# A 4096-row weighted table sum with its two matmul operands exchanged, and its result scaled straight out of PSUM

## The chip, the cores and the metric

The kernel runs on one core of one Trainium2 chip. The metric is device time in microseconds of one execution, median of three runs.

## The reference

The reference is a small audio network on x of shape (128, 256, 64): a depthwise convolution with normalisation, a bilinear attention, a product-key memory layer with causal attention, a linear attention, and a mixture of eight experts. The change touches the memory layer alone. For each of 128 tokens and 8 heads it scores 2 x 64 sub-keys, takes the best 16 of the 4096 sums, and adds up table rows with softmax weights:

```
final_scores, pk_idx = jax.lax.top_k(score, FINAL_TOPK)
final_indices = jnp.take_along_axis(index, pk_idx, axis=-1)
final_scores = jax.nn.softmax(final_scores, axis=-1)
k = jnp.einsum('bnhk,bnhkd->bnhd', kv_scores, keys_table[ind])
v = jnp.einsum('bnhk,bnhkd->bnhd', kv_scores, values_table[ind])
```

A table row is 128 wide here, 64 numbers of the key beside 64 of the value.

## The kernel before, in words

The batch of 128 is worked off as 64 pairs. Three heads of eight are gathered: GpSimd fetches the 16 rows of a token by indirect DMA and VectorE weighs them. The other five heads are dense: all 4096 rows of the head's table take part, each with the weight exp(score) or zero. The 4096 rows are 32 chunks of 128, so a pair has 5 x 32 = 160 chunks, called beats.

Chunks go in twos. For two chunks TensorE runs `ranks` (L1414, two f16 matmuls into a bank `p_s`), ScalarE cuts off what is not chosen (L1169), TensorE adds the exponents (`exponents`, L1423), ScalarE writes exp of the bank into `ew` (L1174), a tile of 128 table rows x (2 batches x 128 tokens). Nine beats later (`LAG`) `product` (L1436) multiplies: the table chunk (128 rows x 128) is the weight operand, the 256 columns of `ew` stream past it, and the sum over 32 chunks grows in bank `p_d` as (128 table columns) x (256 tokens). One f32 matmul call is two weight loads and two matmul instructions in the trace.

When a head's 32 chunks are in, `empty` (ScalarE, L1180) copies `p_d` to SBUF (`dense_t_sb`) and so frees it; the next head's first product waits for that. Some beats later `cross` (TensorE, L1443) transposes both batches' halves into bank `p_g`, and `keep_dense` (ScalarE, L1188) scales each by `fin_r`, one factor per token, and writes it to `kv`.

`p_g` is shared: three times per head `prepare` fills it (L1378, L1388, L1397) with the maps of a later head, ScalarE copies each fill to `mov` (L1158, L1160), and the transposes are the fourth user. All users count one semaphore, `bank_free`; `bank_use` works out at which count each may begin.

Every engine runs its own instructions strictly in a written order. Each piece of work (front, select, prep, tail, back, weigh, sums, dense) is a generator that yields due times in beats, and `interleave` always emits the piece that is due first. In one period the dense heads of a pair run beside `back` of the pair before (attention, linear attention, experts), `select` of the pair ahead, and `front` of the one after that. `BACK` spreads the steps of `back` evenly from `TAIL_END + 1` to beat 155. A period has 80 twos of chunks. Lines used below: L1521 is probabilities times values, L1542 to L1544 the query, key and value products of the linear attention, L1554 its product with `l1_a` (VectorE, L996), L1559 its output product with the expanded `prob_t` (VectorE, L1001), L1277 the ScalarE logarithm of the last variance `b_var` (VectorE, L1027). VectorE's L915 and L922 build one-hot rank tiles of 128x2048 and 128x1024, L943 adds gathered rows.

Of the kernel before, what the change touches and what calls it, by code (L numbers as in the profile page):

```python
# [21 lines left out]
PAIRS = B // 2  # L22
# [72 lines left out]
TAIL_END = LAG + 6  # L95
# [68 lines left out]
def after_dense(d):  # L164

    ready = CHUNKS * (d + 1) + LAG
    return ready + 0.7, ready + 3.25

BANK_ORDER = [k for _, k in sorted([(after_dense(d)[1] % BEATS, ("dense", d)) for d in range(DENSE)]
                                   + [(at_fill(d, i), ("map", 3 * d + i))
                                      for d in range(DENSE) for i in range(3)])]


def bank_use(pair, kind, k):


    at = BANK_ORDER.index((kind, k))  # L180
    period = pair.n + (kind == "dense" and k == DENSE - 1) - (kind == "map" and k < 3)
    before = 2 + len(BANK_ORDER) * period + at
    if not isinstance(period, int):
        return before
    if period < 0:
        return k
    if period == 0:
        return before + (at <= BANK_ORDER.index(("dense", DENSE - 1)))
    if period == PAIRS - 1:
        return before - sum(BANK_ORDER.index(("map", i)) < at for i in range(3))  # L190
    return 2 + len(BANK_ORDER) * period - 3 if period == PAIRS else before

# [12 lines left out]
def over_pairs(eng, front, select, prep, tail, back, weigh, sums, dense):  # L205
# [3 lines left out]
    def period(own, before, ahead, later):  # L209
# [11 lines left out]
        if own is not None:  # L221
            chains += [weigh(own), sums(own), dense(own)]
# [19 lines left out]
def build(nc, x, rows, conv_m, attn_w_src, wqpk_t, keys_t, wq, table, wo, wqkv, wout, wr, w1, b1_t, w2, dense_t, out):  # L242
# [107 lines left out]
    dense_t_sb = sb("dense_t_sb", [128, 2 * T])  # L350
# [111 lines left out]
    dense_tr = sem("dense_tr")  # L462
# [203 lines left out]
    def _(dve):  # L666
# [423 lines left out]
        over_pairs(dve, front, select, prep, nothing, back, weigh, nothing, nothing)  # L1090

    @block.scalar
    def _(act):
# [83 lines left out]
        def empty(pair, d):  # L1177

            act.wait_ge(product_done, BEATS * pair.n + CHUNKS * (d + 1))
            A.copy(dense_t_sb[:, :], p_d[:, 0:2 * T]).then_inc(dense_out_ready, 1)  # L1180

        def keep_dense(pair, d):
            if d == 0:
                act.wait_ge(kv_w_ready, pair.n + 1)
            act.wait_ge(dense_tr, DENSE * pair.n + d + 1)
            for p in range(2):
                g = HEADS * p + GATHERED + d
                last = A.activation(kv[pair.par][:, p, :, GATHERED + d, :],  # L1188
                                    p_g[:, 128 * p:128 * p + 128].rearrange("t (s c) -> t s c", s=2), ACT.Copy,
                                    scale=fin_r[pair.par][:, g:g + 1])  # L1190
            last.then_inc(bank_free, 1)

        def dense(pair):
            for u in range(TWOS):
# [6 lines left out]
                if d > 0 and past == 0:  # L1201
                    yield after_dense(d - 1)[0]
                    empty(pair, d - 1)

        def tail(pair):
            yield BEATS - 2 + EXP_AT - BEATS
            exponent(pair, TWOS - 1)
            yield after_dense(DENSE - 1)[0] - BEATS
            empty(pair, DENSE - 1)
            yield after_dense(DENSE - 1)[1] + 1.15 - BEATS  # L1210
# [4 lines left out]

        def sums(pair):
            for kind, k in BANK_ORDER:
                if kind == "dense" and k < DENSE - 1:
                    yield after_dense(k)[1] + 1.15
                    keep_dense(pair, k)  # L1220
# [75 lines left out]
        over_pairs(act, front, select, prep, tail, back, nothing, sums, dense)  # L1296

    @block.tensor
    def _(pe):
# [66 lines left out]
        def prepare(pair, d):  # L1366
            def fill(part):
                use = bank_use(pair, "map", 3 * d + part)
                if positive(use):
                    hold(pe, bank_free, use)  # L1370
# [35 lines left out]
        def ranks(pair, u):  # L1406
            d, k = divmod(2 * u, CHUNKS)
            if k == 0:
                hold(pe, bank_free, bank_use(pair, "map", 3 * d + 2) + 1)
# [17 lines left out]
        def product(pair, c):  # L1427
# [223 lines left out]
```

## Time and profile before

| | us |
|---|---|
| median of 3 runs | 11342.55 (11342.33 to 11344.62) |
| profiled execution, its time | 11344.7 |
| its span, first to last instruction | 11343.0 |
| TensorE matmuls busy | 10198.0 |
| weight loads busy | 8003.0 |
| VectorE busy | 8728.9 |
| ScalarE busy | 7603.9 |
| TensorE idle for ScalarE's L1169 | 275.0 |
| TensorE idle before L1443 | 127.2 |

Busy time is the union of the intervals in which an engine has something under way. A matmul instruction is shown with its whole passage through the array, so back to back matmuls overlap in the record, and the distance from one start to the next tells their price rather than the length of one. In the page a line of the costliest groups gives count, total busy time, mean length of one, and the idle time of the engine just before them with what ended it.

### The profile page before, as it was taken

How to read it: one execution, taken by the hardware profiler on the slowest of the kernel's cores; microseconds unless marked ns; L12 is line 12 of the kernel's file. 1: busy time of each engine (PE TensorE's matmuls, PEld its weight loads, DVE VectorE, ACT ScalarE, POOL GpSimd, SP SyncE). 2: the span in 40 equal slices, each digit the busy share in tenths (PEclk: the TensorE clock that was granted, in tenths of full speed). 3: DMA queues.
4: the chain of work that ended last, by engine and by line, in shares of the span. 5: the costliest groups of instructions: out<-in, count | busy, mean ns of one | idle time of the engine just before them, and what ended most of it. 6: DMA issues, size and time to landing. Idle time of an engine off the chain costs nothing.

```text
span 11343.0 us, 281179 instructions
## 1 busy us (share of the span) xinstructions
PE 10198.0 (90%) x72608; PEld 8003.0 (71%) x72608; DVE 8728.9 (77%) x41793; ACT 7603.9 (67%) x17491; POOL 6186.2 (55%) x6186
## 2 busy tenths in 40 slices
PE   5998989989999899999998999999999989989998
PEld 4777767777777677777777777777777777777776
DVE  7877778778777787787777877777778778777783
ACT  4666666666666666666666666666666666666665
POOL 5555555555555555555555555555555555555553
PEclk9999999999999999999999999999999999999998
DMA  2333333333333333333333333333333333333332
GB/s 77 100 99 98 100 97 100 100 97 101 99 99 101 97 101 98 99 100 98 99 99 99 100 98 99 99 99 98 99 100 99 99 99 99 99 99 98 99 99 69
DMA packets 603820, 1108.58 MB, mean 98 GB/s; under 512 B 158672, under 2 KB 175568, under 8 KB 602192
## 3 DMA queue, kind: packets, MB, share of 16 engines
q1 hardware_dynamic: 405328, 686.35, 19.0%
q0 software_dynamic: 196608, 403.05, 14.2%
q8 instruction: 714, 11.70, 0.4%
q14 instruction: 882, 7.23, 0.2%
q10 hardware_dynamic: 288, 0.27, 0.0%
HBM read 1084.90 MB, written 4.19 MB: 96 GB/s over the span
## 4 chain that ended last, share of the span: by engine, by line
PE 54%; DVE 19%; ACT 15%; issue 7%; DVEq 4%; ACTq 1%; POOL 0%; DMA 0%; POOLq 0%
PE p_d L1436 20%; PE p_s L1414 6%; PE p_g L1378 5%; PE p_s L1423 5%; ACT ew L1174 4%; ACT p_s L1169 3%; DVE gath L943 3%; PE p_f L1362 2%; ACT prob L1242 2%; PE p_x L1585 2%; PE p_x L1521 2%; PE p_x L1578 2%; DVE rank_hot L915 1%; PE p_x L1507 1%; PE p_x L1514 1%
## 5 line engine op out<-in xcount | busy, mean ns | idle before, releaser
L654 POOL DMA_INDIRECT gath<-in_table,idx x6144 | 6161.9, 1003 | 5033.8 <-PE p_d L1436 3894.5
L1436 PE MATMUL p_d<-ew,tab 128*128 128x256 f32 x20480 | 5715.2, 390 | 11.5 <-ACT dense_t_sb L1180 4.2
L1169 ACT ACTIVATE p_s<-p_s 128x512 f32<-128x512 f32 x5120 | 3053.4, 596 | 2677.1 <-PE p_s L1414 2638.4
L1436 PEld LDWEIGHTS p_d<-ew,tab 128*128 128x128 f32 x20480 | 3411.4, 193 | 377.3 <-issue 46.5
L1174 ACT ACTIVATE ew<-p_s 128x512 f32<-128x512 f32 x5120 | 3077.0, 601 | 151.1 <-PE p_s L1423 149.6
L1423 PE MATMUL p_s<-mov,piece_sel 128*128 128x256 f16 x10240 | 1966.1, 274 | 284.8 <-ACT p_s L1169 275.0
L1414 PE MATMUL p_s<-mov,rank_sel 128*128 128x256 f16 x10240 | 1972.7, 275 | 47.2 <-issue 38.2
L1414 PEld LDWEIGHTS p_s<-mov,rank_sel 128*128 128x128 f16 x10240 | 966.1, 100 | 830.7 <-issue 279.4
L943 DVE SCALAR_TENSOR_TENSOR gath<-gath,kv_w 128x128 f32<-128x128 f32 x4608 | 1310.4, 346 | 64.2
L1423 PEld LDWEIGHTS p_s<-mov,piece_sel 128*128 128x128 f16 x10240 | 956.8, 98 | 533.2 <-issue 397.9
L915 DVE TENSOR_TENSOR rank_hot<-iota_k,rank_key 128x2048 f16<-128x2048 f16 x640 | 777.2, 1223 | 84.7 <-issue 72.1
L1378 PEld LDWEIGHTS p_g<-ident_rank,rank_hot 128*128 128x128 f16 x10240 | 675.6, 103 | 174.2 <-issue 96.6
L1378 PE MATMUL p_g<-ident_rank,rank_hot 128*128 128x128 f16 x10240 | 731.2, 229 | 50.0 <-ACT kv L1188 45.6
L755 DVE MAX8 top<-sim 128x8 f32<-128x64 f32 x2048 | 291.6, 212 | 569.1 <-ACT sim L1144 568.0
L922 DVE TENSOR_TENSOR rank_hot<-rank_hot,rank_val 128x1024 f16<-128x1024 f16 x640 | 424.3, 688 | 29.4 <-issue 0.9
L763 DVE FIND_INDEX8 top_i<-top,sim 128x8 uint32<-128x64 f32 x2048 | 410.1, 219 | 0.0
L785 DVE FIND_INDEX8 top_i<-top,sim 128x8 uint32<-128x64 f32 x2048 | 407.4, 219 | 2.3 <-issue 0.3
L938 DVE TENSOR_SCALAR gath<-gath,kv_w 128x128 f32<-128x128 f32 x1536 | 340.1, 291 | 83.3 <-DMA gath<-in_table,idx 68.3
L771 DVE MATCH_REPLACE8 sim<-top,sim 128x64 f32<-128x64 f32 x2048 | 403.0, 208 | 0.0
L1242 ACT ACTIVATE prob<-p_x,neg_max 128x128 f32<-128x128 f32 x1024 | 385.6, 409 | 13.5 <-DVE neg_max L962 13.5
L1160 ACT CAST mov<-p_g 128x512 f16<-128x512 f32 x640 | 391.4, 611 | 1.4 <-PE p_g L1388 0.8
L1362 PE MATMUL p_f<-score_w,xh_t 64*128 64x512 f32 x512 | 290.1, 647 | 32.4 <-ACT xh_t L1140 30.0
(238 smaller groups left out, 12024.7 us busy)
## 6 DMA issues: line engine op xcount, KB each, us to landing
tab<-in_dense_t SPq DMA_DIRECT2D x2560, 256.0 KB
gath<-in_table,idx POOLq DMA_INDIRECT x6144
xin<-in_x SPq DMA_DIRECT2D x64, 128.0 KB, 2.2
out<-h_out SPq DMA_DIRECT2D x64, 64.0 KB
row_consts<-in_rows SPq DMA_DIRECT2D x1, 548.0 KB, 4.5
w_sb<-in_w SPq DMA_DIRECT2D x1, 512.0 KB, 6.2
w_sb<-in_w ACTq DMA_DIRECT2D x1, 256.0 KB, 4.8
gath<-in_wqpk_t SPq DMA_DIRECT2D x1, 256.0 KB, 5.7
```

Source lines behind the costliest of these rows:

```text
L654: G.indirect_dma_start(out=gath[:, slot, k, :], out_offset=None, in_=table[:, :], in_offset=bass.IndirectOffsetOnAxis(ap=idx[pair.par][:, ...
L915: V.tensor_tensor(hots[p].rearrange("t r s c i -> t (r s) c i"), iota_k[:, :].rearrange("t (c i) -> t c i", i=2)[:, None, :, :].to_broadca ...
L922: V.tensor_tensor(hots[p][:, :, 0, :, :], hots[p][:, :, 0, :, :], rank_val[:, DENSE * p + d, :, None, :].to_broadcast([T, TOPK, SUBKEYS // ...
L943: V.scalar_tensor_tensor(rows[:, k, :], rows[:, first + k, :], share[:, first + k:first + k + 1], rows[:, k, :], ALU.mult, ALU.add)
L1169: A.activation(bank[:, :], bank[:, :], ACT.Relu, scale=-STEEP).then_inc(penalty_ready, 1)
L1174: A.activation(ew[:, slot:slot + 2, :].rearrange("m c t -> m (c t)"), p_s[u % PS_RING][:, :], ACT.Exp, scale=-1.0).then_inc(weights_ready, 1)
L1242: last = A.activation(prob[:, a, hp, :], px[:, a, T * hp:T * hp + T], ACT.Exp, bias=neg_max[:, h:h + 1], accum_out=row_sum[:, a, hp:hp + 1])
L1362: M(p_f[:, :], xh2_t[pair.par][lanes(p), :], score_w[lanes(p), 512 * s:512 * s + 512], start=True, stop=True).then_inc(sim_mm, 1)
L1378: last = M(p_g[:, T * p:T * p + T], rank_hot[p][:, r, :, :].rearrange("t s i -> t (s i)"), ident_rank[:, r, :], start=(r == 0), stop=(r == ...
L1414: last = M(p_s[u % PS_RING][:, 2 * T * i:2 * T * i + 2 * T], rank_sel[:, k + i, :], mov[mov_slot(d)][:, 0, :], start=(i == 0), stop=False, ...
L1423: last = M(p_s[u % PS_RING][:, 2 * T * i:2 * T * i + 2 * T], piece_sel[:, k + i, :], mov[mov_slot(d)][:, MAP_OF[layout], :], start=False, ...
L1436: M(p_d[:, 0:2 * T], tab[:, u % TAB_RING, i, :], ew[:, c % EW_RING, :], start=(k == 0), stop=(k == CHUNKS - 1)).then_inc(product_done, 1)
```

## The change

The operands of the dense product are exchanged. The weight operand is now `ew`, 128 table rows x 128 tokens of one batch, and the table chunk with its 128 columns streams past it. So there is one call per batch, two calls per chunk, each with 128 moving columns; the semaphore is raised once per chunk as before. `p_d` then holds (128 tokens) x (2 batches x 128 table columns), which is the orientation of `kv`. `keep_dense` scales out of `p_d` into `kv` at the place where `empty` stood, and its last instruction is what the next head's first product waits for. `empty`, `cross`, the generator `sums`, `dense_t_sb`, the semaphore `dense_tr` and the transposes' turns in `p_g` are gone. `TAIL_END` becomes `LAG + 2`, so `back` starts four beats earlier and its steps are spread over 143 beats instead of 139.

```diff
-TAIL_END = LAG + 6
+TAIL_END = LAG + 2
 def after_dense(d):
-    ready = CHUNKS * (d + 1) + LAG
-    return ready + 0.7, ready + 3.25
+    return CHUNKS * (d + 1) + LAG + 0.7
+def fills_before(pair, d, part):
+    return 3 * DENSE * pair.n + 3 * d + part
...
-        def empty(pair, d):
-            act.wait_ge(product_done, BEATS * pair.n + CHUNKS * (d + 1))
-            A.copy(dense_t_sb[:, :], p_d[:, 0:2 * T]).then_inc(dense_out_ready, 1)
-
         def keep_dense(pair, d):
             if d == 0:
                 act.wait_ge(kv_w_ready, pair.n + 1)
-            act.wait_ge(dense_tr, DENSE * pair.n + d + 1)
+            act.wait_ge(product_done, BEATS * pair.n + CHUNKS * (d + 1))
             for p in range(2):
                 g = HEADS * p + GATHERED + d
                 last = A.activation(kv[pair.par][:, p, :, GATHERED + d, :],
-                                    p_g[:, 128 * p:128 * p + 128].rearrange("t (s c) -> t s c", s=2), ACT.Copy,
+                                    p_d[:, KV * p:KV * p + KV].rearrange("t (s c) -> t s c", s=2), ACT.Copy,
                                     scale=fin_r[pair.par][:, g:g + 1])
-            last.then_inc(bank_free, 1)
+            last.then_inc(dense_out_ready, 1)
...
             if k == 0 and positive(DENSE * pair.n + d):
                 hold(pe, dense_out_ready, DENSE * pair.n + d)
-            M(p_d[:, 0:2 * T], tab[:, u % TAB_RING, i, :], ew[:, c % EW_RING, :], start=(k == 0),
-              stop=(k == CHUNKS - 1)).then_inc(product_done, 1)
-
-        def cross(pair, d):
-            hold(pe, dense_out_ready, DENSE * pair.n + d + 1)
-            hold(pe, bank_free, bank_use(pair, "dense", d))
-            for p in range(2):
-                last = TR(p_g[:, 128 * p:128 * p + 128], dense_t_sb[:, T * p:T * p + T], ident[:, :])
-            last.then_inc(dense_tr, 1)
+            for p in range(2):
+                last = M(p_d[:, KV * p:KV * p + KV], ew[:, c % EW_RING, T * p:T * p + T], tab[:, u % TAB_RING, i, :],
+                         start=(k == 0 and p == 0), stop=(k == CHUNKS - 1), skip_group_check=True)
+            last.then_inc(product_done, 1)
```

Three places in the engines' orders, first before and then after. Line numbers are those of each kernel: L1436 became L1401 (the product), L1378 became L1342, L1414 L1378, L1423 L1387, L1333 L1298. TensorE from the first product of the next head on, at the end of a pair's second dense head, before:

```order
L1436 MATMUL p_d<-ew,tab 128x256
L513 REGISTER_ALU
L1378 MATMUL p_g<-ident_rank,rank_hot 128x128 x16
L1414 MATMUL p_s<-mov,rank_sel 128x256 x2
L513 REGISTER_ALU
L1423 MATMUL p_s<-mov,piece_sel 128x256 x2
L1436 MATMUL p_d<-ew,tab 128x256 x2
L1333 MATMUL p_f<-f_mv,mean_w 128x2
L513 REGISTER_ALU
L1443 MATMUL p_g<-ident,dense_t_sb 128x128 x2
L1414 MATMUL p_s<-mov,rank_sel 128x256 x2
```

and after:

```order
L1401 MATMUL p_d<-tab,ew 128x128 x2
L491 REGISTER_ALU
L1342 MATMUL p_g<-ident_rank,rank_hot 128x128 x16
L1378 MATMUL p_s<-mov,rank_sel 128x256 x2
L491 REGISTER_ALU
L1387 MATMUL p_s<-mov,piece_sel 128x256 x2
L1401 MATMUL p_d<-tab,ew 128x128 x4
L1298 MATMUL p_f<-f_mv,mean_w 128x2
L1378 MATMUL p_s<-mov,rank_sel 128x256 x2
L491 REGISTER_ALU
L1387 MATMUL p_s<-mov,piece_sel 128x256 x2
```

The transposes are gone from between L1333 and the next ranks, and one product call per chunk has become two of half the width.

ScalarE at the end of the third dense head. Before, with L1169 the cut, L1174 the exponentials, L1180 the copy, L1158 the fill's copy, L1188 the scaling:

```order
L1179 REGISTER_ALU
L1180 COPY dense_t_sb<-p_d 128x256
L1168 REGISTER_ALU
L1169 ACTIVATE p_s<-p_s 128x512
L1174 ACTIVATE ew<-p_s 128x512
L1155 REGISTER_ALU
L1158 ACTIVATE mov<-p_g,rank_off 128x256
L1168 REGISTER_ALU
L1169 ACTIVATE p_s<-p_s 128x512
L1174 ACTIVATE ew<-p_s 128x512
L1185 REGISTER_ALU
L1188 ACTIVATE kv<-p_g,fin_r 128x2x64 x2
```

and after, where L1161 is the scaling, L1147 the cut, L1152 the exponentials and L1136 the fill's copy:

```order
L1158 REGISTER_ALU
L1161 ACTIVATE kv<-p_d,fin_r 128x2x64 x2
L1146 REGISTER_ALU
L1147 ACTIVATE p_s<-p_s 128x512
L1152 ACTIVATE ew<-p_s 128x512
L1133 REGISTER_ALU
L1136 ACTIVATE mov<-p_g,rank_off 128x256
L1146 REGISTER_ALU
L1147 ACTIVATE p_s<-p_s 128x512
L1152 ACTIVATE ew<-p_s 128x512
```

The scaling has moved from two cuts later to the place of the copy.

VectorE some twenty beats later, where `l_a` (L996) and `prob_t` (L1001) are made for TensorE. Before:

```order
L834 TENSOR_TENSOR cand_i<-sim 128x16x4
L913 REGISTER_ALU
L915 TENSOR_TENSOR rank_hot<-iota_k,rank_key 128x2048
L834 TENSOR_TENSOR cand_i<-sim 128x16x3
L834 TENSOR_TENSOR cand_i<-sim 128x16x6
L834 TENSOR_TENSOR cand_i<-sim 128x16x8
L996 SCALAR_TENSOR_TENSOR l_a<-p_x,k_inv,blocks 128x128
...
L853 TENSOR_TENSOR sim<-iota_c,pos_h 128x2496
L922 TENSOR_TENSOR rank_hot<-rank_hot,rank_val 128x16x64 x2
L1001 TENSOR_TENSOR prob_t<-p_x,head_of 128x1024
```

and after (L974 makes `l_a`, L979 makes `prob_t`, L893 and L900 are the rank tiles):

```order
L812 TENSOR_TENSOR cand_i<-sim 128x16x4
L974 SCALAR_TENSOR_TENSOR l_a<-p_x,k_inv,blocks 128x128
L891 REGISTER_ALU
L893 TENSOR_TENSOR rank_hot<-iota_k,rank_key 128x2048
L812 TENSOR_TENSOR cand_i<-sim 128x16x3
L812 TENSOR_TENSOR cand_i<-sim 128x16x6
L812 TENSOR_TENSOR cand_i<-sim 128x16x8
...
L831 TENSOR_TENSOR sim<-iota_c,pos_h 128x2496
L979 TENSOR_TENSOR prob_t<-p_x,head_of 128x1024
L900 TENSOR_TENSOR rank_hot<-rank_hot,rank_val 128x16x64 x2
```

`l_a` now stands ahead of one large rank tile and three candidate adds, and `prob_t` ahead of the two multiplications of the rank tiles. TensorE's L1554 and L1559 themselves stand about one product earlier after the change.

## Rows read from the trace of the kernel before

**Rows 1.** The page of the profiled execution: span, and busy us (share of span) xinstructions.

```profile
span 11343.0 us, 281179 instructions
...
PE 10198.0 (90%) x72608; PEld 8003.0 (71%) x72608; DVE 8728.9 (77%) x41793; ACT 7603.9 (67%) x17491; POOL 6186.2 (55%) x6186
```

**Rows 2.** TensorE groups by line: out<-in shapes xcount | busy us, mean ns | idle before.

```profile
L1436 PE MATMUL p_d<-ew,tab 128*128 128x256 f32 x20480 | 5715.2, 390 | 11.5 <-ACT dense_t_sb L1180 4.2 <-issue 2.1
...
L1521 PE MATMUL p_x<-kv,prob_t 128*128 128x64 f32 x2048 | 246.6, 274 | 2.5 <-ACT prob_t L1248 2.5
...
L1443 PE MATMUL p_g<-ident,dense_t_sb 128*128 128x128 f32 x640 | 127.5, 281 | 127.2 <-ACT mov L1158 126.5 <-ACT dense_t_sb L1180 0.7
```

**Rows 3.** TensorE's waits: who waited for whom, us in total, times, longest.

```profile
PE p_s L1423 <- ACT p_s L1169: 275.0, 315, 2.4
PE p_x L1559 <- DVE prob_t L1001: 129.3, 63, 2.3
PE p_g L1443 <- ACT mov L1158: 126.5, 192, 1.0
PE p_x L1554 <- DVE l_a L996: 105.4, 63, 1.7
...
PE p_g L1378 <- ACT kv L1188: 45.6, 63, 0.8
```

**Rows 4.** Timeline of TensorE at one head's end: start us, us, engine line op.

```profile
5067.55 0.67 PE L1436 MATMUL p_d<-ew,tab 128*128 128x256 f32 x2
5068.06 1.06 PE L1378 MATMUL p_g<-ident_rank,rank_hot 128*128 128x128 f16 x16
5068.95 0.38 PE L1414 MATMUL p_s<-mov,rank_sel 128*128 128x256 f16 x2
...
5069.39 1.03 PE L1436 MATMUL p_d<-ew,tab 128*128 128x256 f32 x4
5070.26 0.28 PE L1333 MATMUL p_f<-f_mv,mean_w 128*128 128x2 f32 x2
5071.43 0.41 PE L1443 MATMUL p_g<-ident,dense_t_sb 128*128 128x128 f32 x2 [0.89 <-ACT mov L1158]
5071.67 0.38 PE L1414 MATMUL p_s<-mov,rank_sel 128*128 128x256 f16 x2
```

**Rows 5.** Timeline of ScalarE over the same stretch.

```profile
5066.55 0.59 ACT L1174 ACTIVATE ew<-p_s 128x512 f32<-128x512 f32 x1
5067.03 0.38 ACT L1180 COPY dense_t_sb<-p_d 128x256 f32<-128x256 f32 x1
5069.37 0.58 ACT L1169 ACTIVATE p_s<-p_s 128x512 f32<-128x512 f32 x1 [1.96 <-PE p_s L1414]
5069.87 0.59 ACT L1174 ACTIVATE ew<-p_s 128x512 f32<-128x512 f32 x1
5070.34 0.30 ACT L1110 ACTIVATE b_log<-b_mv,eps_ln 128x2 f32<-128x2 f32 x1
5070.71 0.20 ACT L1112 ACTIVATE b_rstd<-b_log 128x2 f32<-128x2 f32 x1
5070.82 0.46 ACT L1158 ACTIVATE mov<-p_g,rank_off 128x256 f16<-128x256 f32 x1
5072.09 0.58 ACT L1169 ACTIVATE p_s<-p_s 128x512 f32<-128x512 f32 x1 [0.81 <-PE p_s L1414]
5072.58 0.59 ACT L1174 ACTIVATE ew<-p_s 128x512 f32<-128x512 f32 x1
5073.06 0.63 ACT L1188 ACTIVATE kv<-p_g,fin_r 128x128 f32<-128x128 f32 x2
```

**Rows 6.** Timeline of TensorE, 128-column f32 matmuls back to back.

```profile
5077.60 0.39 PE L1543 MATMUL p_x<-xh_t,wqkv_sb 128*128 128x128 f32 x2
5077.82 0.39 PE L1544 MATMUL p_x<-xh_t,wqkv_sb 128*128 128x128 f32 x2
5078.05 0.60 PE L1436 MATMUL p_d<-ew,tab 128*128 128x256 f32 x2
```

**Rows 7.** Weight loads (PEld) by line, same columns as rows 2.

```profile
L1436 PEld LDWEIGHTS p_d<-ew,tab 128*128 128x128 f32 x20480 | 3411.4, 193 | 377.3 <-issue 46.5
...
L1521 PEld LDWEIGHTS p_x<-kv,prob_t 128*128 128x128 f32 x2048 | 246.7, 194 | 8.1 <-issue 3.4
```

**Rows 8.** VectorE groups of the page: xcount | busy us, mean ns | idle before.

```profile
L943 DVE SCALAR_TENSOR_TENSOR gath<-gath,kv_w 128x128 f32<-128x128 f32 x4608 | 1310.4, 346 | 64.2
...
L915 DVE TENSOR_TENSOR rank_hot<-iota_k,rank_key 128x2048 f16<-128x2048 f16 x640 | 777.2, 1223 | 84.7 <-issue 72.1
...
L922 DVE TENSOR_TENSOR rank_hot<-rank_hot,rank_val 128x1024 f16<-128x1024 f16 x640 | 424.3, 688 | 29.4 <-issue 0.9
```

**Rows 9.** ScalarE's waits.

```profile
ACT b_log L1277 <- DVE b_var L1027: 148.5, 63, 2.6
```

**Rows 10.** Busy us of the engines in three stretches around L1559's wait, granted clock (PEclk).

```profile
5080.00:5098.00 18.00, 13.38 (x83) 10.34 (x80) 16.68 (x64) 11.95 (x27) 13.19 (x12) 1.00 0.42 117
5098.00:5106.30 8.30, 7.99 (x69) 7.17 (x70) 7.68 (x15) 0.37 (x1) 1.59 (x2) 0.59 0.17 49
5106.30:5120.00 13.70, 12.10 (x83) 9.12 (x80) 9.63 (x33) 9.87 (x23) 9.15 (x9) 1.00 0.35 98
```

**Rows 11.** Mean granted clock of the execution.

```profile
core 0: 11343.0 us, clock 0.980
```

More of the change, by code:

```diff
@@ L164, in after_dense @@
 def after_dense(d):
-    ready = CHUNKS * (d + 1) + LAG
-    return ready + 0.7, ready + 3.25
[L172 to L191, printed above, removed]
+    return CHUNKS * (d + 1) + LAG + 0.7
+def fills_before(pair, d, part):
+    return 3 * DENSE * pair.n + 3 * d + part
 def interleave(*chains):
@@ L202, in interleave, with over_pairs @@
         nearest[0] = next(nearest[1], None)
-def over_pairs(eng, front, select, prep, tail, back, weigh, sums, dense):
+def over_pairs(eng, front, select, prep, tail, back, weigh, dense):
     def period(own, before, ahead, later):
@@ L221, in period @@
         if own is not None:
-            chains += [weigh(own), sums(own), dense(own)]
+            chains += [weigh(own), dense(own)]
         interleave(*chains)
@@ L1089, in _ @@
         V_sync()
-        over_pairs(dve, front, select, prep, nothing, back, weigh, nothing, nothing)
+        over_pairs(dve, front, select, prep, nothing, back, weigh, nothing)
     @block.scalar
@@ L1201, in dense @@
                 if d > 0 and past == 0:
[L1202 to L1203 removed]
+                    yield after_dense(d - 1)
+                    keep_dense(pair, d - 1)
         def tail(pair):
@@ L1294, in back @@
             A.preload_act_table_set("natural_log_exp_and_others")
-        over_pairs(act, front, select, prep, tail, back, nothing, sums, dense)
+        over_pairs(act, front, select, prep, tail, back, nothing, dense)
     @block.tensor
@@ L1367, in fill @@
             def fill(part):
-                use = bank_use(pair, "map", 3 * d + part)
-                if positive(use):
-                    hold(pe, bank_free, use)
+                if positive(fills_before(pair, d, part)):
+                    hold(pe, bank_free, fills_before(pair, d, part))
             for p in range(2):
@@ L1464, in tail @@
                 product(pair, c)
-            yield after_dense(DENSE - 1)[1] - BEATS
-            cross(pair, DENSE - 1)
-        def sums(pair):
-            for kind, k in BANK_ORDER:
-                if kind == "dense" and k < DENSE - 1:
-                    yield after_dense(k)[1]
-                    cross(pair, k)
         def back(pair):
@@ L1485, in back @@
             yield BACK["k_tr"]
-            hold(pe, bank_free, bank_use(pair, "dense", DENSE - 1) + 1)
+            hold(pe, dense_out_ready, DENSE * count)
             hold(pe, summed, 2 * GATHERED * count)
@@ L1589, in nothing @@
             return iter(())
-        over_pairs(pe, front, select, prep, tail, back, nothing, sums, dense)
+        over_pairs(pe, front, select, prep, tail, back, nothing, dense)
     ctx.close()
```

13 lines of the change are left out of this document (2 added, 11 removed).

## The prediction

> **What bounds the kernel now.** I read the page first, then TensorE's groups by line, then its waits, then the timeline at a head's end. TensorE has a matmul under way in 10,198 of 11,343 us; no other engine is above 77% [rows 1]. Half of that is the dense product, 5,715 us in L1436 [rows 2]. So time is TensorE's instruction stream plus its 1,145 us of idleness (11,343 − 10,198), and the stream is written in a fixed order, so each wait is one instruction that holds up all behind it. The dearest waits are short and repeat in every pair: for ScalarE's cut 275 us, for two VectorE results 129 and 105, before the transposes 126.5, before a map fill 45.6 [rows 3]. The reader is to see that starts, not lengths, price a matmul: four instructions of L1436 start at 5069.39 and the next line starts at 5070.26, so 0.87 us for four, 0.435 us per call, although each is shown 0.39 long [rows 2, 4].
>
> **The product itself (+150 us).** There are 10,240 calls with 256 moving columns (20,480 instructions), each 0.435 us. After the change there are 20,480 calls with 128 columns: as many columns, but four weight loads per chunk for two. The same shape (f32, 128x128 weights, 128 columns) runs back to back in L1543 and L1544: two instructions from 5077.60 to 5077.82, two more to 5078.05, so 0.225 per call, 0.45 per chunk [rows 6]. That is 0.015 more per chunk, times 10,240: +154, taken as +150. Bounds: L1521, in which 64-column matmuls leave the weight load as the pace, has 246.6 us for 2,048, 0.120 each [rows 2], four make 0.48, +0.047 per chunk, +480 us. From below, sixteen of L1521 in a long run would show a little less than 0.11 apiece when the tail is taken off, which makes the product free: 0. I take [rows 6], since they are this very shape.
>
> A rule of the Trainium skill bears on this. The loads of L1436 are under way 3,411 us for 20,480, 0.167 each [rows 7]. "Perfetto Trace Analysis", section "Identifying the Most-Contended Engine", says that matmul busy time is no good measure and that the busy share of weight loads is to be judged instead. By it the loads, now 71%, would go to 8,003 + 3,411 − 74 = 11,340 us, the whole span, and the change would be bad. The trace agrees only in part: L1521's loads, packed, are under way 0.120 each (246.7 for 2,048), so the 0.167 is stretched by the matmul in front.
>
> **The hand-over of the bank (+60 us).** The next head's first product waits until `p_d` is read. Before, one copy: 5067.03 to 5067.41, and the product starts at 5067.55 [rows 4, 5]. I read the 0.14 as the way of the signal, not as slack. Now the two scalings stand there; as a pair they take 0.63 against 0.38 [rows 5], so the product is 0.25 later. Behind it on TensorE stand sixteen rank matmuls and everything else. Four heads of five look so; in the fifth ScalarE sits idle before the copy and TensorE runs slowly, which I cost at nothing. 256 x 0.25 = +64, taken as +60; if 0.14 were slack 256 x 0.11 = 28; if all five, 80.
>
> **The transposes (−75 us) and their waits (−126 us).** L1443 starts at 5071.43 and the next line at 5071.67: 0.24 a head [rows 4], times 320 = 75 us. Before it TensorE waited 126.5 us in 192 cases, three heads of five, for ScalarE's L1158 to empty the shared bank [rows 3]; the timeline shows why: products end, ScalarE is still at L1169, L1174, two roots and L1158, which starts at 5070.82 and ends at 5071.28 [rows 5]. With no turn of the transposes in the bank, TensorE goes on to ranks, whose bank is free. The next user of the shared bank comes some four calls later.
>
> **The fill that waited for the scaling (−46 us).** L1378 waited 45.6 us, 63 times up to 0.8, for L1188 [rows 3]. L1188 no longer touches that bank. What is late next is the rank tile of VectorE; that is in none of the dear waits, so I take all of it. Bounds of both removed waits: nothing to all.
>
> **What the earlier start of `back` moves (−110 us).** VectorE makes `l_a` now ahead of one L915, 1.22 us [rows 8], and some adds. TensorE waited for it 1.67 us in each pair (105.4 / 63) [rows 3], and arrives a product, 0.43, earlier (my estimate from the order; a call is 0.435): 63 x (1.22 − 0.43) = 50. `prob_t` is ahead of two L922, 1.38 us; the wait was 2.05 us (129.3 / 63); 63 x (1.38 − 0.43) = 60. Bounds: 0, and both waits whole, 235.
>
> **What comes back (+61 us).** In about 20 of the 80 twos, from the key and query products to L1277, VectorE sets the pace (the waits of [rows 3, 9] lie there). Products dearer by 0.015 cost nothing in it: a quarter of 150, −37. But what TensorE gains at `l_a` and `prob_t` is partly met again at L1277, where ScalarE waits 148.5 us for VectorE's `b_var` [rows 9] and holds up the next cut. That wait moves one two earlier on ScalarE (1.31 us of TensorE's time: 0.44 for ranks and exponents from 5068.95 to 5069.39, and 0.87 for two products) [rows 4], while `b_var` loses four L943, 1.38 us, ahead of it. So it stays as long as it is, and I let half of the 110 come back: +55. Of the two removed bank waits (172) I let a quarter return at the cut of L1169: +43.
>
> **The rest.** ScalarE loses 320 copies of 0.38, 121 us of 7,604; it idles a third of the time, so nothing. The gathers and table loads count the same semaphore once per chunk as before: nothing.
>
> **Sum** on the profiled execution: 150 + 60 − 75 − 126 − 46 − 110 + 61 = −86. Its own time is 11,344.7, 1.7 above its span and 2 above the median. 11,342.5 − 86 gives 11,257; I say 11,260.
>
> A second rule would sharpen the first term. Per load and matmul the trace shows 0.112 [rows 6]. "TensorE: Matmul & The Clock Gate", section "LDWEIGHTS (loading the stationary operand)", gives a load as its columns over 1.2 per ns, 107 ns for 128. By it, as an estimate, a chunk would cost 0.427, no more than before, and the sum would end at about 11,100. The measured row decides, and it is 5 ns apiece above it.
>
> **Rivals.**
> - *Everything removed is kept, and the clock stays up.* After the wait for `prob_t` the granted clock falls to its 1.2 GHz level: 0.59 on the mean over 5098.0 to 5106.3, 1.00 on both sides [rows 10]. The whole run has 0.980 [rows 11], so 2% of 11,343, 227 us, of TensorE's time are lost to it. If the shorter waits at L1554 and L1559 keep it at 2.4 GHz in half the pairs, and nothing comes back, the time is 11,260 − 70 − 60 = 11,130. For it: the fall stands right behind the two longest waits. [...] Chance 0.22.
> - *Slower: the waits come back while the loads stay.* A wait for a bank is only where a late ScalarE or VectorE shows. If they are late whatever TensorE does, it meets them one step on, at L1387 (the old L1423), and of the gains only the transposes' own 75 are left: 150 + 60 − 75 − 37 = +98: about 11,440. It decides the sign once more than 184 of the 282 us (126 + 46 + 110) return; 98 are already let back in the forecast. For it: the order of `back` against the fills of the bank has changed, and the eight exponentials of the second attention now start nearer to a head's end, where the scalings are. Against it: ScalarE catches up within a two, 0.97 us from one cut to the end of the exponentials' turn (5069.37 to 5070.34) [rows 5] against 1.30. Chance 0.19.
> - *Loads pace the product at 0.120.* +480 for +150: about 11,590. Against it [rows 6]. Chance 0.04.
> - *No change.* The same, with just those 184 returned: 11,342. Chance 0.11.
>
> **How the numbers follow.** My forecast, with 11,190 to 11,318, has 0.44. What a measurement tells from no change is 0.2%, 23 us. Faster by more: 0.44 + 0.22 and a little of the sum's tails, 0.68. Within: 0.11. Slower: 0.21. The range reaches from the clock rival to nearly the slower one: 11,090 to 11,420.
>
> **What would show it.** Right: L1401 with 40,960 instructions whose fours of calls take 0.90 from start to next start; TensorE idle before it for L1161 or a gap of 0.25 more at each head's first product; no idle of 0.9 between L1298 and L1378; the wait for `l_a` under 60 us in total and for `prob_t` under 80; weight loads under way near 9,200 us and not 11,300. Wrong: waits at L1387 grown by more than 150 us, a start distance of 0.12 per load in L1401, or a mean clock below 0.980.

## The result, and the profile after

The changed kernel takes 11,660.4 us (median of four runs), the one before 11,342.4: ratio 1.0284, interval 1.0266 to 1.0302. I had forecast 11,260 and "faster" at 0.68. It is 2.8% slower, and above my range of 11,090 to 11,420.

The page of the kernel after, its first line and its line of busy times:

```profile
span 11661.2 us, 319239 instructions
...
PE 10409.8 (89%) x92448; PEld 9373.4 (80%) x92448; DVE 8731.9 (75%) x41793; ACT 7583.3 (65%) x17171; POOL 6251.0 (54%) x6186
```

Beside [rows 1] TensorE is busy 212 us more and idle 106 us more. Two groups of part 5, the product's matmuls and its weight loads:

```profile
L1401 PE MATMUL p_d<-tab,ew 128*128 128x128 f32 x40960 | 5961.0, 283 | 131.4 <-ACT kv L1161 122.7
L1401 PEld LDWEIGHTS p_d<-tab,ew 128*128 128x128 f32 x40960 | 5253.4, 196 | 320.6 <-issue 204.1
```

TensorE's waits after (for whom, us in total, times, longest us):

```profile
PE p_x L1454 <- DVE k_t L948: 220.9, 64, 3.5
PE p_x L1510 <- DVE prob_t L979: 158.5, 63, 2.9
PE p_f L1305 <- DVE xh L667: 151.8, 64, 29.9
PE p_d L1401 <- ACT kv L1161: 122.7, 148, 3.1
PE p_s L1387 <- ACT p_s L1147: 121.4, 317, 2.1
PE p_x L1516 <- DVE xn L1015: 88.2, 63, 6.2
...
PE p_x L1505 <- DVE l_a L974: 40.2, 63, 0.7
```

Beside [rows 3] three things went as forecast: no wait is left before transposes, next to none before the map fill (3.3 us for 45.6), and `l_a` fell from 105.4 to 40.2. But one row is new and the dearest of all: 221 us in 64 pairs for `attn_o`, the first attention's result, which lies in the buffer that the rows call `k_t`. Before, it was a wait in one pair, of 0.9 us. (In the same way `prob_t` at L1510 is `l1_x`, the expanded tile of the linear attention.)

Where in a pair the time went, I read by measuring from one pair of rank matmuls to the next (L1414 before, L1378 after), 80 such steps ("twos") a pair, mean over 58 pairs (the fourth to the 61st). A table of sums in us worked out from the traces; the columns beside the first and last are experiments, told below:

```
twos     before  e3     j3     e1     e4    after
0-3       8.47   9.54   8.69   9.20   9.37   9.39
4-7       9.52   9.58   8.62   8.72  10.33  10.34
8-11      8.54   8.65   8.54   8.65   7.03   7.03
12-19    15.66  15.66  15.67  15.66  19.21  22.42
20-24    12.92  13.00  12.74  12.82  11.49  11.81
25-35    22.66  22.82  22.66  22.83  22.14  22.13
36-38     7.33   7.37   6.31   6.38   7.88   7.88
39-47    13.80  14.01  13.80  14.01  13.93  13.95
48-52    17.76  18.20  18.83  17.86  17.85  18.02
53-60    12.54  12.63  11.24  11.46  12.56  12.57
61-70    21.49  21.48  20.46  20.56  20.43  20.32
71-79    23.84  24.12  24.13  24.01  23.98  24.00
pair    174.54 177.07 171.70 172.16 176.20 179.83
```

After against before, +5.3 us a pair, and one stretch holds it: twos 12 to 19 take 6.8 more (earlier work of `back` stands there too, so a part is only moved from later twos). There the timeline of VectorE shows, after:

```profile
5154.51 0.20 DVE L749 MATCH_REPLACE8 sim<-top,sim 128x64 f32<-128x64 f32 x1
5156.93 0.20 DVE L944 RECIPROCAL row_inv<-row_sum 128x8 f32<-128x8 f32 x1 [2.22 <-ACT prob L1207]
5157.28 1.23 DVE L893 TENSOR_TENSOR rank_hot<-iota_k,rank_key 128x2048 f16<-128x2048 f16 x1
...
5158.83 0.60 DVE L758 MAX8 top<-sim 128x8 f32<-128x64 f32 x4
...
5169.53 0.68 DVE L948 TENSOR_TENSOR k_t<-p_x,row_inv 128x512 f32<-128x512 f32 x1
```

and the same place before:

```profile
5017.54 0.21 DVE L771 MATCH_REPLACE8 sim<-top,sim 128x64 f32<-128x64 f32 x1
5017.90 1.23 DVE L915 TENSOR_TENSOR rank_hot<-iota_k,rank_key 128x2048 f16<-128x2048 f16 x1 [0.15 <-issue]
...
5019.44 0.60 DVE L780 MAX8 top<-sim 128x8 f32<-128x64 f32 x4
...
5024.10 0.20 DVE L966 RECIPROCAL row_inv<-row_sum 128x8 f32<-128x8 f32 x1
...
5032.28 0.67 DVE L970 TENSOR_TENSOR k_t<-p_x,row_inv 128x512 f32<-128x512 f32 x1
```

The reader is to see the place of one short instruction. `row_inv`, the reciprocal of the attention's sums, was behind the rank tile, the MAX8s and the weighing of gathered values; when its turn came ScalarE's exponentials were long done. Now it is right behind the MATCH_REPLACE8s, ahead of all that, and VectorE stands idle 2.22 us for ScalarE. Everything behind is late, `attn_o` (L948) last. TensorE at that time, after:

```profile
5166.21 0.61 PE L1401 MATMUL p_d<-tab,ew 128*128 128x128 f32 x4
5170.35 0.59 PE L1454 MATMUL p_x<-causal,ident_bf 128*128 128x512 bf16 x2 [3.53 <-DVE k_t L948]
5170.88 1.82 PE L1458 MATMUL p_x<-k_t,q_t 64*128 64x128 f32 x16
5172.63 1.22 PE L1401 MATMUL p_d<-tab,ew 128*128 128x128 f32 x4
```

And at the same instructions before:

```profile
5033.60 0.38 PE L1423 MATMUL p_s<-mov,piece_sel 128*128 128x256 f16 x2
5033.82 0.59 PE L1503 MATMUL p_x<-causal,ident_bf 128*128 128x512 bf16 x2
5034.35 1.16 PE L1507 MATMUL p_x<-k_t,q_t 64*128 64x128 f32 x16
```

It waits 3.53 us for `attn_o`, and the score products behind it (16 instructions) then take 1.82 us where they took 1.16, and the next four of the product 1.22 where 0.61 is usual: the lower clock. VectorE's own waits, after:

```profile
DVE row_inv L944 <- ACT prob L1207: 673.3, 128, 12.4
DVE top L733 <- ACT sim L1122: 344.0, 128, 8.1
```

Before, the first of these (L966) was 91.4 us. The granted clock over the run is 0.962 (0.980 before, [rows 11]); summed over the trace's stretches at the lower level that is 887 us in place of 463.

### The profile page after: what moved, and what is told of

Same layout as the page of the kernel before. It is cut to its first block, busy times and chain, and to the rows that moved or that the text cites. A ratio compares the mean times of both kernels' runs of the same rounds, so it can differ in the third digit from the quotient of the medians.

```text
span 11661.2 us, 319239 instructions
## 1 busy us (share of the span) xinstructions
PE 10409.8 (89%) x92448; PEld 9373.4 (80%) x92448; DVE 8731.9 (75%) x41793; ACT 7583.3 (65%) x17171; POOL 6251.0 (54%) x6186
## 4 chain that ended last, share of the span: by engine, by line
PE 38%; DVE 34%; ACT 12%; issue 9%; DVEq 7%; ACTq 0%; POOL 0%; POOLq 0%
PE p_d L1401 14%; DVE gath L921 6%; PE p_s L1378 4%; ACT ew L1152 4%; DVE rank_hot L893 3%; PE p_s L1387 3%; PE p_g L1342 3%; ACT prob L1207 3%; ACT p_s L1147 2%; PE p_x L1536 2%; DVE top_i L763 2%; PE p_f L1327 2%; PE p_x L1458 2%; PE p_x L1529 1%; DVEq L923 1%
## 5 line engine op out<-in xcount | busy, mean ns | idle before, releaser
L632 POOL DMA_INDIRECT gath<-in_table,idx x6144 | 6226.8, 1013 | 5287.7 <-PE p_d L1401 4203.9
L1401 PE MATMUL p_d<-tab,ew 128*128 128x128 f32 x40960 | 5961.0, 283 | 131.4 <-ACT kv L1161 122.7
L1401 PEld LDWEIGHTS p_d<-tab,ew 128*128 128x128 f32 x40960 | 5253.4, 196 | 320.6 <-issue 204.1
L1147 ACT ACTIVATE p_s<-p_s 128x512 f32<-128x512 f32 x5120 | 3044.7, 595 | 3263.3 <-PE p_s L1378 3239.8
L1152 ACT ACTIVATE ew<-p_s 128x512 f32<-128x512 f32 x5120 | 3077.5, 601 | 89.2 <-PE p_s L1387 85.3
L1387 PE MATMUL p_s<-mov,piece_sel 128*128 128x256 f16 x10240 | 1994.9, 277 | 121.8 <-ACT p_s L1147 121.4
L1378 PE MATMUL p_s<-mov,rank_sel 128*128 128x256 f16 x10240 | 2000.9, 278 | 43.4 <-issue 35.8
L1387 PEld LDWEIGHTS p_s<-mov,piece_sel 128*128 128x128 f16 x10240 | 981.1, 99 | 360.5 <-issue 227.8
L1378 PEld LDWEIGHTS p_s<-mov,rank_sel 128*128 128x128 f16 x10240 | 987.4, 102 | 312.5 <-issue 247.7
L893 DVE TENSOR_TENSOR rank_hot<-iota_k,rank_key 128x2048 f16<-128x2048 f16 x640 | 776.5, 1222 | 92.8 <-issue 64.9
L1342 PE MATMUL p_g<-ident_rank,rank_hot 128*128 128x128 f16 x10240 | 714.3, 226 | 3.4 <-DVE rank_hot L900 3.3
L1342 PEld LDWEIGHTS p_g<-ident_rank,rank_hot 128*128 128x128 f16 x10240 | 665.9, 102 | 15.4 <-issue 4.5
L944 DVE RECIPROCAL row_inv<-row_sum 128x8 f32<-128x8 f32 x128 | 26.0, 204 | 673.3 <-ACT prob L1207 673.3
L900 DVE TENSOR_TENSOR rank_hot<-rank_hot,rank_val 128x1024 f16<-128x1024 f16 x640 | 423.6, 687 | 24.7 <-issue 0.9
```

The lines of the kernel that those rows point to most:

```text
L632: G.indirect_dma_start(out=gath[:, slot, k, :], out_offset=None, in_=table[:, :], in_offset=bass.IndirectOffsetOnAxis(ap=idx[pair.par][:, ...
L893: V.tensor_tensor(hots[p].rearrange("t r s c i -> t (r s) c i"), iota_k[:, :].rearrange("t (c i) -> t c i", i=2)[:, None, :, :].to_broadca ...
L900: V.tensor_tensor(hots[p][:, :, 0, :, :], hots[p][:, :, 0, :, :], rank_val[:, DENSE * p + d, :, None, :].to_broadcast([T, TOPK, SUBKEYS // ...
L1147: A.activation(bank[:, :], bank[:, :], ACT.Relu, scale=-STEEP).then_inc(penalty_ready, 1)
L1152: A.activation(ew[:, slot:slot + 2, :].rearrange("m c t -> m (c t)"), p_s[u % PS_RING][:, :], ACT.Exp, scale=-1.0).then_inc(weights_ready, 1)
L1342: last = M(p_g[:, T * p:T * p + T], rank_hot[p][:, r, :, :].rearrange("t s i -> t (s i)"), ident_rank[:, r, :], start=(r == 0), stop=(r == ...
```

## The experiments

Theory A: the earlier start of `back` (TAIL_END from LAG + 6 to LAG + 2) changes which instruction stands ahead of which in the in-order streams of VectorE and ScalarE, and these waits, with the clock that falls behind them, are the loss. Theory B: the loss is the product's doubled weight loads and the hand-over of `p_d`. Each time below is the median beside the kernel before on the same chip (11,341 to 11,350), with the ratio to it.

**e1, `back` at its old place.**

```diff
-TAIL_END = LAG + 2
+TAIL_END = LAG + 6
```

> The changed kernel with TAIL_END = LAG + 6, as before the change, so that `back` (second attention, router, outputs) starts four places later and only the turned product, the scalings into kv and the missing copy and transposes are left of the change. Theory A (the loss is made by the earlier `back`: VectorE's in-order stream then has the reciprocal row_inv at L944 ahead of the selection's work, idles for ScalarE's exponentials, and delivers attn_o late to TensorE's L1454): 11,280 to 11,340, TensorE's wait for k_t at L1454 under 30 us (221 in the changed kernel), row_inv's wait for ScalarE under 150 us (673), granted clock 0.975 or more. Theory B (the loss is made by twice the weight loads and the two scalings at each head's end): the time stays at 11,600 to 11,660.

11,178.4 us, ratio 0.9853 (0.9836 to 0.9869). TensorE's waits:

```profile
PE p_s L1387 <- ACT p_s L1147: 253.1, 316, 3.3
PE p_x L1510 <- DVE prob_t L979: 115.6, 59, 2.2
PE p_x L1505 <- DVE l_a L974: 107.3, 63, 1.9
...
PE p_d L1401 <- ACT kv L1161: 49.0, 205, 1.1
```

No wait above 1.3 us is left at L1454, `row_inv` waits 91 us, time at the lower clock is 506 us. B is out: this kernel has all its loads and scalings. The shift of `back` costs 482 us, and everything else in the change gains 167, so the time lies below even A's range. (`TAIL_END` moves the start of `back` and, since its end stays, stretches its steps from 139 to 143 beats; no run parts the two.)

**e2, only the shift, in the kernel before.**

```diff
-TAIL_END = LAG + 6
+TAIL_END = LAG + 2.5
```

> The kernel before with TAIL_END = LAG + 2.5 in place of LAG + 6 and nothing else (2 itself would put the transpose of the second attention's keys ahead of the cross product it needs). Theory A: about as much is lost as the whole change lost and a little more, since nothing is gained beside it: 11,600 to 11,720, with a new wait of TensorE for k_t at the second scores of 150 to 250 us and a granted clock under 0.970. Theory B: 11,340, within 40. If both the earlier start and the turned product are needed for the loss (A with the scalings on ScalarE making the exponentials late), 11,350 to 11,500.

11,970.5, ratio 1.0552 (1.0531 to 1.0574): +625. Two of TensorE's waits:

```profile
PE p_x L1503 <- DVE k_t L970: 231.4, 64, 3.7
...
PE p_x L1493 <- ACT kv L1188: 134.8, 64, 2.3
```

And one of VectorE's:

```profile
DVE row_inv L966 <- ACT prob L1242: 710.7, 128, 12.8
```

The same wait for `attn_o` appears without the turned product, as A said, but the time is 250 us above its range. One part of that A had not in it: the fifth head's sums are not in `kv` when the transposes of the keys (L1493) want them, 2.1 us a pair, and twos 4 to 7 take 12.46 us for 9.52. With the scalings straight out of `p_d` that wait is 1.3 us in the whole run; so the change removes one obstacle to an earlier `back`, but does not make it good.

**e3, only the doubled loads, in the kernel before.** A call of 256 columns is cut in two of 128 with the same weights:

```diff
-            M(p_d[:, 0:2 * T], tab[...], ew[:, c % EW_RING, :], start=(k == 0), ...)
+            for p in range(2):
+                last = M(p_d[:, T * p:T * p + T], tab[...], ew[:, c % EW_RING, T * p:T * p + T], ...)
```

> The kernel before with each dense call of 256 moving columns cut into two of 128 with the same table weights: the results, the copy, the transposes and the order are as before; only the weight loads per chunk go from two to four, as in the changed kernel. My forecast's term: 0.015 per chunk, +150, of which up to a quarter hidden under VectorE: 11,450 to 11,500, with four calls' instructions 0.90 us from start to start at full clock. Theory B: +300 or more, 11,640 and above.

11,491.6, ratio 1.0132 (1.0115 to 1.0149): +146, the forecast's term (150). Twos without anything else go from 1.302 to 1.330 us, +0.014 a chunk. But the column e3 of the table shows that the total is not this price times 10,240. Twos 12 to 19 and 61 to 70, where other waits set the pace, did not grow at all. And of the 2.53 us a pair, 1.01 stand at two 0 alone, in every fourth pair only (7.7 us for 3.6), and 0.46 at two 52; TensorE's time at the lower clock is 117 us for 41 at twos 0 to 3, and 269 for 210 at twos 48 to 52. Summed over all 64 pairs that is 59 us at two 0, 23 at two 52, and 68 everywhere else.

**e4, one VectorE instruction moved, in the changed kernel.**

```diff
-                yield BACK[f"p_tr{p}"]
+                yield BACK[f"o{p}"] - 0.05
                 dve.wait_ge(prob_ready, 2 * done + p + 1)
                 V.reciprocal(row_inv[...], row_sum[:, :, :])
```

> The changed kernel with one VectorE instruction moved per attention: the reciprocal row_inv goes from the place of the transposes of the probabilities to just ahead of attn_o, its only reader, so that the selection's twelve or more instructions stand ahead of the wait for ScalarE's sums. Theory A: row_inv's wait for ScalarE falls from 673 to under 250 us, TensorE's wait for k_t at L1454 from 221 to under 100, the time to 11,350 to 11,480. Rival A2 (VectorE's backlog is the work ahead of attn_o itself, not the idle time before the reciprocal): attn_o comes as late as before, 11,600 to 11,660. Theory B: 11,660.

11,437.2, ratio 1.0082 (1.0065 to 1.0099): 223 of the 482 us come back by moving 128 instructions of 0.2 us. `row_inv` waits 5.9 us in all now. TensorE's wait for `attn_o`:

```profile
PE p_x L1454 <- DVE k_t L948: 85.0, 63, 2.3
```

VectorE's own at the same tile:

```profile
DVE k_t L948 <- PE p_x L1472: 127.6, 64, 6.8
```

The first went from 221 to 85; VectorE now waits at `attn_o` itself, for TensorE, so the chain is still early for it. TensorE's busy time fell by 103 us with the same instructions in it, and its time at the lower clock from 887 to 652.

**f1, g2, g3: how late.** TAIL_END = LAG + 4, LAG + 8, and LAG + 6 with e4's edit.

> The changed kernel with TAIL_END = LAG + 4, half way between the changed kernel (LAG + 2, 11,660) and the one at 11,178 (LAG + 6). By the order, row_inv now stands behind the first rank tile, the pieces and four MAX8s, so the wait theory puts it much nearer the good end: row_inv's wait for ScalarE 150 to 350 us (673 and 91 at the ends), TensorE's wait for k_t at L1454 30 to 100 (221 and none), time 11,230 to 11,370. If the loss goes in proportion to the shift and not to which instruction stands ahead of which: 11,400 to 11,440.

> The changed kernel with TAIL_END = LAG + 8, two places later than the best one yet. The wait theory says that at LAG + 6 the attention finds VectorE's orders already right and no wait at L1454 is left, so there is little to gain: 11,140 to 11,200. Rival: the later start squeezes the routers and outputs against the pair's end, and waits there grow: 11,220 to 11,300.

> The changed kernel with both: TAIL_END = LAG + 6 and the reciprocal just ahead of attn_o. If moving the reciprocal helps only through its wait, which is 91 us at LAG + 6 and hides nobody's wait, nothing changes: 11,160 to 11,195. If it gives VectorE back real time: 11,100 to 11,150.

11,267.6 (0.9925, 0.9908 to 0.9941), 11,217.5 (0.9880, 0.9863 to 0.9896), 11,187.9 (0.9856, 0.9839 to 0.9872). A row of TensorE's waits at LAG + 4:

```profile
PE p_x L1454 <- DVE k_t L948: 112.8, 64, 2.0
```

And one at LAG + 8:

```profile
PE p_x L1505 <- DVE l_a L974: 236.1, 63, 3.9
```

Half of the shift undone gives back 81% of the loss, so it goes by the order and not in proportion. The wait at L1454 was above my 100 and that of `row_inv`, 55 us, below my 150. Later than LAG + 6, `l_a` is late (236 us in place of 107): the time lies between my two ranges, 2.5 us under the rival's, whose mechanism is the one that shows; "little to gain" was wrong. Moving the reciprocal at LAG + 6 gives nothing, since its wait hides nobody's.

**h1, the wait filled.** Is the clock a part of the price of a wait, or a companion?

```diff
                 else:
+                    for _ in range(13):
+                        M(p_d[:, 256:384], ident[:, :], wq_sb[:, 0:128], start=False, ...)
                     hold(pe, attn_o_ready, 2 * done + 1)
```

> The changed kernel (11,660) with thirteen matmuls of no use (f32, 128 columns, into the unused half of p_d's bank) put ahead of TensorE's wait for attn_o at L1454. They take about 13 times 0.225, 2.9 us, of a wait that is 3.45 us in each pair, so they lengthen nothing. If TensorE's idleness is what lets the clock fall to its lower level behind that wait, the clock stays up behind it and 0.5 to 1.5 us a pair come back: 11,560 to 11,630, granted clock from 0.962 to 0.966 or more. If the idle time has no part in it: 11,660. If the thirteen are not hidden: 11,700 to 11,850.

11,576.0, ratio 1.0191 (1.0174 to 1.0208): 1,664 instructions more, 84 us less. The wait, now at L1457:

```profile
PE p_x L1457 <- DVE k_t L948: 38.8, 62, 0.6
```

The core's span and granted clock:

```profile
core 0: 11576.4 us, clock 0.972
```

In the changed kernel a stretch at the lower level began at this place in 56 of 58 pairs; with TensorE kept busy, in none. Twos 12 to 19 take 21.39 us for 22.42 and twos 20 to 24 11.53 for 11.81, 1.31 a pair or 84 us; what changed elsewhere adds up to nothing (0.85 less at twos 48 to 52, 0.63 more at 61 to 70).

**i1, i2, the same for the waits that are left in e1**, eight useless matmuls ahead of L1510's wait, and in i2 six more ahead of L1505's.

> The kernel at 11,178 (the changed one with TAIL_END = LAG + 6) with eight matmuls of no use (f32, 128 columns, unused half of p_d's bank) ahead of TensorE's wait for l1_x (the tile prob_t, L1510), 8 x 0.225 = 1.8 us of a wait that is 1.96 us in 59 pairs. Of this kernel's 506 us at the lower clock 215 stand right behind this wait, in 40 of 64 pairs. If the idleness lets the clock fall, as the filled wait at L1454 showed, half of these 215 come back at most: 11,070 to 11,140 with the low-clock time down to 290 to 400 us. If the clock falls there for the few columns that the z products stream: 11,178, within 20.

> The same and six more such matmuls ahead of the wait for l_a (L1505), 1.35 us of a wait that is 1.7 us in 63 pairs. Only 14 us at the lower clock stand behind that wait, so filling it should give nothing: within 20 us of the kernel that fills only l1_x's. If each filled wait shortens the low time by itself, however little stands behind it, 20 to 60 less.

11,177.6 (0.9848, 0.9834 to 0.9861) and 11,165.7 (0.9838, 0.9825 to 0.9852). My expectation of i1 failed although its mechanism worked: time at the lower clock fell from 506 to 391 us, and twos 48 to 52 from 17.86 to 16.35; twos 61 to 70 went from 20.56 to 21.50. The time is the one that its second case names, but not for that case's reason: the same z products follow, and with the idle time ahead of them filled the time at the lower clock fell from 236 to 20 us at twos 48 to 52. The row that took it, TensorE's wait for the cut (253.1 in e1):

```profile
PE p_s L1387 <- ACT p_s L1147: 305.3, 317, 3.3
```

And behind it ScalarE's wait for `b_var` (150.9 in e1):

```profile
ACT b_log L1242 <- DVE b_var L1005: 202.1, 63, 3.7
```

TensorE is faster there only to wait for ScalarE, which waits for VectorE: the same filling is worth 84 us at L1454 and nothing here. i2 lies 12 us below i1, within its first case.

**j2, j3: the two other terms, on top of e1.** j2 has one copy for the two scalings and leaves out the weights `fin_r`; j3 has the product of before, and leaves out the transposition that its sums would need.

```diff
-            for p in range(2):
-                last = A.activation(kv[...], p_d[:, KV * p:KV * p + KV]..., ACT.Copy, scale=fin_r[...])
+            last = A.copy(kv[pair.par][:, :, :, GATHERED + d, :], p_d[:, 0:2 * KV]...)
```

> The kernel at 11,178 with the two scalings of a head's sums on ScalarE (0.63 as a pair) made one copy of 256 columns (0.38), that leaves the weights fin_r out. Prices the hand-over of the bank: my forecast's term was 0.25 a head at 256 heads, +60 for the two scalings against a copy, so 11,100 to 11,130 here. If the next head's first product does not wait for ScalarE so closely (slack): 11,150 to 11,180.

> The kernel at 11,178 with the product of before (table stationary, 256 columns moving, two weight loads a chunk) in place of the turned one. The sums then lie the other way round and are scaled as they lie, so the transposition is left out: it is the kernel before with only the copy, the transposes and their bank turns taken away. With the measured price of the doubled loads, +146, it should be 11,030 to 11,050; the removed things together then are worth 11,342 less that, about 300, where my forecast had 126 + 75 + 46 - 60 = 187. If the turned product was dearer or cheaper here than in the split kernel: outside 11,010 to 11,070.

11,166.3 (0.9841, 0.9827 to 0.9854) and 11,148.2 (0.9818, 0.9804 to 0.9831). Neither came out as in its first case. j2's time lies in its second range (slack behind the scalings), but slack is not what the twos show; j3's is outside 11,010 to 11,070, so the doubled loads are cheaper here than in e3. In j2 the 0.25 us is there, at twos 4, 20 and 36 exactly (3.326 for 3.577 and so on), 0.75 a pair or 48 us; 0.26 come back at 48 to 52 and 0.21 at 0 to 3, so the run moves by only 12. In j3 every plain two is 0.028 shorter than in e1, and the gain again goes at one place: twos 48 to 52 take 18.83 for 17.86, with 321 us at the lower clock in 50 pairs there where e1 has 215 in 40. At twos 0 to 3, j3 is 0.51 shorter than e1. So an edit worth 146 us in one kernel is worth about 30 in the other: the price of a plain two is the same, and the waits and the lower clock at two 0 and twos 48 to 52 add to it in the one and take from it in the other.

**k1, k5, k7: what e4 left.** ScalarE in e4 at the second head's end:

```profile
4937.17 0.29 ACT L1088 ACTIVATE b_log<-b_mv,eps_ln 128x2 f32<-128x2 f32 x1 [1.15 <-DVE b_mv L661]
...
4937.64 0.58 ACT L1147 ACTIVATE p_s<-p_s 128x512 f32<-128x512 f32 x1
...
4938.63 0.61 ACT L1161 ACTIVATE kv<-p_d,fin_r 128x128 f32<-128x128 f32 x2
```

TensorE at that place:

```profile
4939.39 0.35 PE L1401 MATMUL p_d<-tab,ew 128*128 128x128 f32 x1 [1.60 <-ACT kv L1161]
```

This `b_log` belongs to the normalisation behind the second attention. It is one more waiting instruction that came ahead: of the cut, the exponential and the scalings. At LAG + 2 its due place is 72.8 and that of the scalings 73.7; at LAG + 4 it is 74.0, behind them. k1 is e4 with it moved behind:

```diff
-            yield BACK["root1"]
+            yield max(BACK["root1"], after_dense(1) + 0.1)
```

> The changed kernel with the reciprocal moved (11,437) and one more step moved: ScalarE's root1 of `back` (b_log, b_rstd at L1088 and L1090, which wait 1.35 us in each pair for VectorE's b_mv, 87 us in all) goes behind the cut, the exponential and the two scalings of the second head's end. In the wait theory TensorE's first product of the next head, which waited 1.6 us there for the scalings, finds them done: its wait falls from 133 to 40 to 60 us, and the time to 11,330 to 11,370. If another engine is as late there, for instance the rank tile or the map fill behind it: 11,420 to 11,440. Slower, 11,450 or more, if the router's chain, now later, holds up the queries behind it.

> The changed kernel with TAIL_END = LAG + 5. At LAG + 4 TensorE still waited 113 us for attn_o at L1454 (11,268), at LAG + 6 not at all (11,178). If the wait shrinks evenly: 11,200 to 11,240. If LAG + 5 already has VectorE's order of LAG + 6: 11,170 to 11,190.

> The changed kernel with TAIL_END = LAG + 7. Between LAG + 6 (11,178) and LAG + 8 (11,217, with the wait for l_a at 236 us instead of 107): 11,180 to 11,210. Below 11,165 it would be the best of them and my reading of LAG + 6 as the meeting point wrong.

k1: 11,397.6 (1.0050, 1.0033 to 1.0066). TensorE's wait for the scalings fell from 133.0 to

```profile
PE p_d L1401 <- ACT kv L1161: 44.8, 194, 1.1
```

88 us less, as expected, of which 40 arrive at the end: 0.5 us a pair are met again right behind, at two 38, and 0.3 at twos 61 to 70. So my range for the time was too low. k5 (LAG + 5): 11,173.0 (0.9851, 0.9835 to 0.9868), level with LAG + 6 as in the second case; a wait of 46.3 us at L1454 is left in it, and costs nothing that shows in the total. k7 (LAG + 7): 11,221.1 (0.9893, 0.9877 to 0.9910), a little above my range. The best place is LAG + 5 or + 6, and both beat the kernel before by 1.5%.

## Why the prediction was wrong

**The failing step is "What the earlier start of `back` moves (−110 us)".** Its sign was wrong: it costs 482 us (e1 against the changed kernel), 592 from what I took. The step looked only at the two results of `back` that TensorE had been waiting for, `l_a` and `prob_t`, and asked how much sooner VectorE gets to them. It never asked what `back`'s own first instructions wait for when they come four places sooner: `row_inv` for ScalarE (91 to 673 us), `attn_o` behind it. `attn_o` had 0.9 us among TensorE's waits before, and the 91 of `row_inv` cost TensorE nothing, so I gave them no price, while its bounds (0 to 235) held no loss at all. Of its two halves `l_a` held (−65 for −50), `prob_t` did not: 158.5 for 129.3.

**The slower rival** had its place nearly right ("the order of `back`", "the exponentials of the second attention nearer a head's end") and its mechanism and price wrong: it let gains come back to at most +98, and it blamed ScalarE's load. What k1 found at a head's end is a ScalarE instruction that waits for VectorE: 88 us of TensorE's wait, 40 of the time; what e4 found is VectorE waiting for ScalarE, 223 of the time. Moving these two steps gives back 263 of the 482 us; the rest (219 between k1 and e1) I have only as waits for `xh`, `prob_t`, `prob` and `attn_o` that are longer than in e1. It stands at twos 12 to 24 (2.2 us a pair more than in e1), 36 to 38 (0.6) and 53 to 60 (1.1), less 0.7 at 25 to 35. No run took it apart, and its cause stays open.

**The product (+150)** came out at +146 alone (e3), partly by luck. The price was right: fours of calls take 0.893 us from start to start, for my 0.90. But of the 143 us that 0.014 a chunk makes, about 68 show, where I let only 37 be hidden. The rest of the 146 stands at two 0 and two 52, where more of the time is at the lower clock, and my sum had nothing for it. The loads' busy time rose to 9,373 us, where I had 9,200 against 11,340 for unshortened loads. In e3 it rose by 1,320 us and the time by 146, so it did not give the price.

By "Perfetto Trace Analysis" in the Trainium skill, section "Identifying the Most-Contended Engine", the loads' busy share is one of two measures to judge TensorE by; here it would have overstated the cost. "TensorE: Matmul & The Clock Gate" in the Trainium skill, section "LDWEIGHTS (loading the stationary operand)", gives 107 ns for a load of 128 columns. The trace nearly agrees: 0.893 / 8 = 0.112 for a load and its matmul. At 0.107 the eight would take 0.856 us, less than the 0.866 of four before, so the 5 ns make the term.

**The hand-over (+60)** was there at three heads of five, 48 us in its place, and worth 12 at the end (j2).

**Transposes, their waits and the fill (−247)**: with the hand-over my forecast is −187, or −144 with the 43 that I let come back, and j3, which has just these, shows −201. Right in size; by the twos, more is gained at 4 to 7, 36 to 38 and 53 to 70 (4.25 us a pair), and 1.07 is lost again at 48 to 52.

**What comes back**: I let half of the gain at `prob_t` return at `b_var`. i1 shows all of it returning. The idea held; it stood in the sum for a gain that was never made.

**The clock** I had as a chance to gain. It was an added loss: 887 us at the lower level for 463 (of my own signs of a wrong forecast, only the mean clock below 0.980 came true; the waits at L1387 fell to 121), and h1 shows 84 us of the run's time to hang on the idle TensorE ahead of `attn_o`.

Without the shift my sum would have been 150 − 37 + 60 − 247 + 43 = −31, and e1 is −167. So of the 404 us by which the whole was off, the shift made 537 (482 for my −110 + 55), and the other terms, 136 too high together, hid a part of that. The two parts of it that were measured alone add up to −55 (+146 and −201); the other 112 are the meeting of the two, most of it at twos 48 to 52 (by the parts 17.76 + 0.44 + 1.07 = 19.27, measured 17.86) and the rest at 0 to 3, which no sum of terms taken apart holds.

## What to carry to other kernels

When a block of work is moved earlier in hand-ordered in-order engines, list for each of its instructions what it waits for, and on which engine it then stands ahead of whom. The dear ones here were short ones that read another engine's result, and TensorE's waits before the change do not show them, since there they cost it nothing. Test a change with two edits in halves: here the halves were −167 and +482. A gain counts only if the next instruction that meets another engine is not met earlier by as much.

## What the chip showed that I had not expected

- A wait of TensorE can cost more than its length: filling 3.45 us of idleness a pair with matmuls of no use kept the granted clock at 1.00, its 2.4 GHz level, at that place in all 58 pairs measured, where it had fallen to the 1.2 GHz level in 56, and made the program 84 us shorter (h1).
- Twice as many f32 weight loads, 20,480 more of 128 columns, cost 146 us in one program (e3) and 30 us in another with other waits (e1 against j3), although a plain two is 0.028 us longer in both.
- The gain of a cured clock can be nothing: i1 has 115 us less at the lower level than e1 and the same time.
